# Transposing softmax probabilities by products with diagonals, or by true transposes with the reciprocals applied to y

## What is computed

```
scores = einsum('bhid,bhjd->bhij', q, k) + einsum('bhid,jd->bhij', q, rel)
scores = where(causal, scores, -inf)
probs  = softmax(scores, axis=-1)
y      = einsum('bhij,bhjd->bhid', probs, v)
out    = y.transpose(0, 2, 1, 3).reshape(b, t, c) @ w_proj + b_proj
```

## Time and profile before

| what | value |
|---|---|
| time, median of 3 runs | 7268.11 us (7267.75 to 7270.31) |
| span of the profiled execution, its own time | 7259.2 us |
| instructions | 167273 |
| PE / PEld busy | 91% / 82% |
| DVE / ACT / POOL busy | 74% / 50% / 43% |
| mean granted clock of TensorE | 0.906 |
| DMA | 24 GB/s over the span |
| products with diagonals (L714) | 1175.1 us of PE, 9216 instructions |
| diagonals (L502) | 608.4 us of POOL, 512 instructions |

### The profile page before, as it was taken

One profiled execution on the slowest core, in us unless ns is written; L12 is line 12 of the kernel. 1 busy time (PEld: TensorE's weight loads), 2 busy tenths in 40 slices (PEclk: granted clock), 3 DMA queues, 4 the chain that ended last, 5 costly groups with the idle time before them and its releaser, 6 DMA issues.

```text
span 7259.2 us, 167273 instructions
## 1 busy us (share of the span) xinstructions
PE 6605.1 (91%) x56000; PEld 5936.7 (82%) x56000; DVE 5383.8 (74%) x15934; ACT 3644.6 (50%) x12160; POOL 3111.4 (43%) x4048
## 2 busy tenths in 40 slices
PE   4999999999999999999999999999999999999998
PEld 4888888888888888888888888888888888888887
DVE  3777777777777777777777777777777777777776
ACT  1545555554555455545545554555455455545554
POOL 4444444444444444444444444444444444444443
PEclk8889899999899998989989998999899999899998
DMA  4211121112111111211121111112111211121110
GB/s 46 29 22 23 22 29 22 23 22 29 22 23 26 25 23 22 27 23 23 22 29 22 23 25 25 23 22 28 23 23 22 29 22 23 22 29 22 23 24 8
DMA packets 228657, 175.83 MB, mean 24 GB/s; under 512 B 27785, under 2 KB 228126, under 8 KB 228630
## 3 DMA queue, kind: packets, MB, share of 16 engines
q1 hardware_dynamic: 218934, 173.46, 18.4%
q10 hardware_dynamic: 8336, 1.07, 0.2%
q0 software_dynamic: 1360, 0.96, 0.1%
HBM read 156.11 MB, written 19.27 MB: 24 GB/s over the span
## 4 chain that ended last, share of the span: by engine, by line
issue 34%; PE 20%; DVE 18%; POOL 15%; POOLq 9%; DVEq 3%; ACT 1%; ACTq 0%
PE bank L693 7%; POOL diag L502 6%; DVE qz L1109 5%; POOL rstd L487 4%; PE bank L645 4%; DVE negmax L1128 2%; DVE z L1062 2%; PE bank L681 2%; POOLq L556 2%; POOL h L557 2%; PE bank L781 2%; POOLq L486 2%; POOL res L565 2%; PE bank L792 2%; POOLq L582 2%
## 5 line engine op out<-in xcount | busy, mean ns | idle before, releaser
L1514 ACT ACTIVATE p<-bank,negmax 98x98 f32<-98x98 f32 (+1 forms) x3072 | 1132.3, 376 | 317.6 <-DVE negmax L1128 274.6
L714 PEld LDWEIGHTS bank<-diag,p 128*98 128x98 f32 x9216 | 1066.0, 202 | 157.1 <-issue 104.0
L714 PE MATMUL bank<-diag,p 128*98 128x98 f32 x9216 | 1175.1, 291 | 14.7 <-POOL diag L502 1.7
L1522 ACT COPY pT<-bank 98x392 f32<-98x392 f32 x768 | 374.7, 488 | 1542.2 <-PE bank L714 1542.1
L693 PE MATMUL bank<-tokw,x_sb 128*98 128x193 f32 x4096 | 924.3, 382 | 9.1 <-DVEq L1049 9.1
L502 POOL TENSOR_TENSOR diag<-ident,rden 98x588 f32<-98x588 f32 x512 | 608.4, 1199 | 648.2 <-DVE rden L1142 648.2
L693 PEld LDWEIGHTS bank<-tokw,x_sb 128*98 128x98 f32 x4096 | 825.0, 260 | 67.5 <-issue 29.2
L1128 DVE TENSOR_REDUCE negmax<-bank 98x1 f32<-98x196 f32 (+2 forms) x1536 | 626.1, 456 | 269.0 <-PE bank L681 268.7
L681 PE MATMUL bank<-qk_parts,qz 128*98 128x196 f32 (+1 forms) x6144 | 744.7, 265 | 0.0
L681 PEld LDWEIGHTS bank<-qk_parts,qz 128*98 128x98 f32 x6144 | 656.8, 166 | 11.4
L520 POOL TENSOR_TENSOR qz<-qk_parts,ones 32x588 fp32r<-32x588 f32 x256 | 301.2, 1176 | 721.8 <-DVE qk_parts L1099 701.5
(11 more groups left out here) (272 smaller groups left out, 14889.4 us busy)
## 6 DMA issues: line engine op xcount, KB each, us to landing
x_sb<-in_x SPq DMA_DIRECT2D x384, 196.0 KB, 4.8
x_sb<-in_x SPq DMA_DIRECT2D x384, 189.0 KB, 8.0
out<-out_row SPq DMA_DIRECT2D x128, 147.0 KB
x_store<-in_L_tok_W SPq DMA_DIRECT2D x6, 96.0 KB
diag<-in_L_ffn_W SPq DMA_DIRECT2D x1, 576.0 KB
gstore<-in_L_ffn_W SPq DMA_DIRECT2D x1, 384.0 KB
p<-in_L_attn_w_attn ACTq DMA_DIRECT2D x2, 96.0 KB
gstore<-in_L_ffn_W ACTq DMA_DIRECT2D x1, 192.0 KB
```

The source lines that it names most:

```text
L714: last = mm(bank[b][0:HT, HT * i:HT * i + HT], src, diag[:, h // 3, t, h % 3], start=True, stop=True)
L1514: sc.activation((p1 if t else p0)[0:HT, 3 * s + g], bank[b][0:HT, c0:c0 + (T if t else HT)], ACT.Exp, bias=negmax[:, s, t, g:g + 1], accum ...
L1522: sc.copy(pt_dst(name[0], int(name[1:])), bank[RING[name]][0:HT, 0:4 * HT]).then_inc(sem["pT_act"], 1)
```

## The change

True transposes take the place of the products with diagonals. The diagonals on POOL (and their tile) go, and with them the four calls that waited for the sums of a slot each. DVE takes all reciprocals at once, after the copy of A0, and copies each 32 times beside itself (rden32, 98 x 768). PE transposes that in six blocks (R0 with four, R1 with two), ACT copies them to rdenT, in which each reciprocal stands in the 32 rows of its slot. In `attention` DVE multiplies y by rdenT to yn, ACT rounds yn instead of y, and DVE makes yparts from these. The ring has two more pieces, A4's copy moves from ACT to DVE, A3 now stands behind R0, and A4 with B1 ahead of the scatter. The semaphores rden_sb and diag_sb go; rden_T, rden32_sb, rdenT_sb and yn_sb are new. PE's A and B pieces now wait for `probs` itself. The tile norm_store takes diag's place, also for the weights that lie there during set-up.

```diff
@@ -54,11 +54,11 @@
-RING = dict(S0=0, S1=1, S2=2, T0=3, S3=0, S4=1, S5=2, S6=0, S7=1, A0=2, A1=0, A2=3, B0=1, A3=2,
-            B1=0, A4=1, A5=3, B2=0)
+RING = dict(S0=0, S1=1, S2=2, T0=3, S3=0, S4=1, S5=2, S6=0, S7=1, A0=2, A1=0, A2=3, B0=1, R0=2,
+            A3=0, B1=1, A4=3, R1=2, A5=0, B2=1)
 ORDER = list(RING)
 PT = [name for name in ORDER if name[0] in "AB"]
-PT_ACT = ("A1", "B0", "B1", "A4", "A5", "B2")
+PT_ACT = ("A1", "B0", "B1", "A5", "B2")
 PAIRS = ((0, 0), (0, 1), (1, 0), (2, 2), (2, 3))
...
@@ -190,7 +190,10 @@
         negmax = sb("negmax", [HT, 4, 2, NG])
         den = sb("den", [HT, 4, 2, NG])
         rden = sb("rden", [HT, 4, 2, NG])
-        diag = sb("diag", [128, 4, 2, NG, HT])
+        norm_store = sb("norm_store", [128, 2 * NG * T + 2 * NG * 128])
+        rdenT, yn = (norm_store[:, i * NG * T:(i + 1) * NG * T].rearrange("p (g t) -> p g t", g=NG)
+                     for i in range(2))
+        rden32 = norm_store[0:HT, 2 * NG * T:].rearrange("p (t g e) -> p t g e", t=2, g=NG)
         p0 = sb("p0", [128, NH, HT])
         p1 = sb("p1", [128, NH, T])
...
@@ -476,8 +479,7 @@
             select(diag_of[:], ALU.is_ge, 0.0, 31, -1, [[32, 4], [0, DH]])
             gp.drain().then_inc(one["consts_made"], 1)
             gp.wait_ge(one["w_ready"], 1)
-            for t in (p1, diag):
-                gp.memset(t[:], 0.0)
+            gp.memset(p1[:], 0.0)
             gp.drain().then_inc(one["p1_zeroed"], 1)
             def rstd(var, ve, r, name):
...
                     gp.tensor_tensor(h1b[:], h1[:], both(bp), ALU.add).then_inc(sem["h1b_sb"], 1)
-
-                def diagonals(s):
-
-                    gp.wait_ge(sem["rden_sb"], after("rden_sb", n, s + 1))
-                    gp.tensor_tensor(
-                        diag[0:HT, s].rearrange("p t g i -> p (t g) i"),
-                        ident[0:HT, 0:HT].unsqueeze(1).broadcast_to([HT, 2 * NG, HT]),
-                        rden[:, s].rearrange("p t g -> p (t g)").unsqueeze(2).broadcast_to(
-                            [HT, 2 * NG, HT]), ALU.mult).then_inc(sem["diag_sb"], 1)
...
@@ -530,8 +523,6 @@
                     gp.drain()
                     gp.tensor_tensor(sqsum[:].unsqueeze(2), x_sq[:, :, 0:1], x_sq[:, :, 1:2],
                                      ALU.add).then_inc(sem["sqsum_sb"], 1)
-                if front:
-                    diagonals(0)
                 if back:
                     gp.wait_ge(sem["sel_sb"], after("sel_sb", m))
...
@@ -539,17 +530,12 @@
-                    diagonals(1)
...
-                    diagonals(2)
-                    diagonals(3)
...
@@ -710,10 +696,20 @@
                     else:
                         blocks = [(4 * k + i, 1, 1) for i in range(4)]
                     for i, (h, t, u) in enumerate(blocks):
-                        src = p1[:, h, HT * u:HT * u + HT] if t else p0[:, h]
-                        last = mm(bank[b][0:HT, HT * i:HT * i + HT], src, diag[:, h // 3, t, h % 3],
-                                  start=True, stop=True)
+                        src = p1[0:HT, h, HT * u:HT * u + HT] if t else p0[0:HT, h]
+                        last = pe.transpose(bank[b][0:HT, HT * i:HT * i + HT], src,
+                                            ident[0:HT, 0:HT])
                     last.then_inc(sem["p_T"], 1)
+
+                def inverse_cols(k, b):
+
+                    for i, g in enumerate(((0, 1), (2,))[k]):
+                        for t in range(2):
+                            last = pe.transpose(
+                                bank[b][:, i * T + t * HT:i * T + t * HT + HT],
+                                rden32[:, t, g],
+                                ident[0:HT, 0:HT])
+                    last.then_inc(sem["rden_T"], 1)
                 def bank_free(name):
...
@@ -726,6 +722,8 @@
                         pe.wait_ge(sem["probs"], after("probs", n, int(o[1:]) + 1))
                     elif o[0] == "T" and head:
                         pe.wait_ge(sem["tok_y"], after("tok_y", l))
+                    elif o[0] == "R":
+                        pe.wait_ge(sem["rdenT_sb"], after("rdenT_sb", n, int(o[1:]) + 1))
                     elif o[0] in "AB":
                         engine, count = evacuation(o)
                         pe.wait_ge(sem[engine], after(engine, n, count))
@@ -742,10 +740,13 @@
                             by = "qz_sb" if k < 4 else "qz2_sb"
                             pe.wait_ge(sem[by], after(by, n, k // 2 % 2 + 1))
                         scores(k, RING[name])
+                    elif kind == "R":
+                        pe.wait_ge(sem["rden32_sb"], after("rden32_sb", n))
+                        inverse_cols(k, RING[name])
                     else:
                         s = (2 * k + 1 if kind == "A" else 4 * k + 3) // 3
-                        pe.wait_ge(sem["diag_sb"], after("diag_sb", n, s + 1))
+                        pe.wait_ge(sem["probs"], after("probs", n, 2 * s + 2))
                         transposes(kind, k, RING[name])
                 def embed(t, q0, q1):
...
@@ -852,6 +853,7 @@
                     pe.wait_ge(sem["pT_dve"], after("pT_dve", n))
                     pe.wait_ge(sem["pT_act"], after("pT_act", n, SEMS["pT_act"] - 1))
+                    pe.wait_ge(sem["rdenT_sb"], after("rdenT_sb", n))
                     for groups in ((0, 1), (2,)):
                         for g in groups:
                             for s in range(4):
...
                 if front:
+                    causal("R0")
                     causal("A3")
                 if back:
                     attn_out()
                 if front:
                     causal("B1")
+                    causal("A4")
                 if back:
                     scatter()
                 if front:
-                    causal("A4")
+                    causal("R1")
                     causal("A5")
                     causal("B2")
                     attention()
...
@@ -1136,10 +1140,15 @@
                     ve.tensor_copy(pt_dst(name[0], int(name[1:])),
                                    bank[RING[name]][0:HT, 0:4 * HT]).then_inc(sem["pT_dve"], 1)
-                def inverse_sums(s):
-
-                    ve.wait_ge(sem["probs"], after("probs", n, 2 * s + 2))
-                    ve.reciprocal(rden[:, s], den[:, s]).then_inc(sem["rden_sb"], 1)
+                def inverse_sums():
+
+                    ve.wait_ge(sem["probs"], after("probs", n))
+                    ve.reciprocal(rden[:], den[:])
+                    ve.drain()
+                    ve.tensor_copy(
+                        rden32.rearrange("p t g (s e) -> p (t g) s e", e=32),
+                        rden[:].rearrange("p s t g -> p (t g) s").unsqueeze(3).broadcast_to(
+                            [HT, 2 * NG, 4, 32])).then_inc(sem["rden32_sb"], 1)
...
@@ -1311,13 +1320,19 @@
                 def attention():
+                    def group(t, g0, gn):
+                        return t[:, g0:g0 + gn].rearrange("p g t -> p (g t)")
+
+                    for i, (g0, gn) in enumerate(((0, 2), (2, 1))):
+                        ve.wait_ge(sem["y_mm"], after("y_mm", n, i + 1))
+                        ve.tensor_tensor(group(yn, g0, gn), bank[2 + i][:, 0:gn * T],
+                                         group(rdenT, g0, gn), ALU.mult).then_inc(sem["yn_sb"], 1)
+                    ve.drain()
                     for i, (g0, gn) in enumerate(((0, 2), (2, 1))):
                         ve.wait_ge(sem["yhi_sb"], after("yhi_sb", n, i + 1))
                         ve.scalar_tensor_tensor(
-                            yparts[:, g0:g0 + gn].rearrange("p g t -> p (g t)"),
-                            yhi[:, g0:g0 + gn].rearrange("p g t -> p (g t)").bitcast(F32),
-                            lo_rows[:], bank[2 + i][:, 0:gn * T], ALU.mult,
-                            ALU.add).then_inc(sem["yparts_sb"], 1)
+                            group(yparts, g0, gn), group(yhi, g0, gn).bitcast(F32), lo_rows[:],
+                            group(yn, g0, gn), ALU.mult, ALU.add).then_inc(sem["yparts_sb"], 1)
                 def mlp_input():
                     ve.wait_ge(sem["h3_rstd"], after("h3_rstd", m))
...
@@ -1384,19 +1398,17 @@
                     mix_pooled()
                 if front:
                     maxima(6)
-                    inverse_sums(1)
                 if back:
                     max2()
                 if head:
                     patch_variance()
                 if front:
                     maxima(7)
-                    inverse_sums(2)
                 if head:
                     embedding()
                 if front:
                     transposed("A0")
-                    inverse_sums(3)
+                    inverse_sums()
                 if back:
                     mix_cols()
                     context2()
...
                     transposed("A3")
+                    transposed("A4")
                 if head:
                     h1_stats()
```

(16 more changed lines are left out.)

12 lines of the change are left out of this document (4 added, 8 removed).

## The result

The changed kernel takes 7146.8 us (median of 4 runs, 7144.6 to 7148.1), the kernel before 7269.0 on the same chip: ratio 0.983, 95% interval 0.9816 to 0.9844. It is faster; the forecast was slower, 7400.

The account below looks back on a forecast made before the run. PE, with its granted clock, was taken to set nearly all of a step's time. Short steps at 54.4 us and long at 56.7, half and half, plus 1.0 for patches: +1.1 x 127 - 2 = +137, 7400 us, own range 7300 to 7510.

Parts of the forecast that it names:

- The three terms of the short step: Mix 1.1 us earlier, A4's copy on DVE +0.46, y times reciprocals before the projection +1.03; together +0.4 us.
- A transpose is one record and 0.09 us: PE: each true transpose of 98 columns is one instruction of 0.09 us, against 0.17 a block for diagonal products.
- the wait for mT: PE's wait for DVE's split of mT ahead of the mix: still some 1.6 us, since PE comes earlier too.
- +2.5 us in a long step: Clock low through the transposes stays low at the projection (1.0 us) and the products behind it (1.5).
- the 1.5 us put on the short steps: One low-clock stretch behind PE's new idleness at the projection, taking short steps to 54.4 us.
- only grow: nothing: PE's waits for y_row's bank and mT grow as transposes before them shorten, so nothing is gained there.
- The short steps: Four of eight neighbouring steps, 52.5 to 54.3 us, clock low only some 3 us after the wait for mT.
- the fast rival: Clock granted as before: -1.0 us a step, 7140 us; chance 0.30.
- My own signs for right and wrong: Right: mean clock under 0.89, low at a later projection. Wrong: clock holds 0.906 or rises, or projection no later.
- My -2.7 for the longest step: From the mix to h2, PE's halved transposes at low clock shorten 17.2 to 15.6 us; with the 1.1, -2.7.
- "The change does not reach" the patches: Low stretch in the patch products, 1.6 us in five steps of eight: 1.0 us a step, before and after.
- The transposes' rule as a rival: Transposes neither raise nor hold the clock, so no step is short: +2.7 us a step, 7610 us; chance 0.17.

Follow-up runs that it names:

- run 13: Kernel before, GpSimd's multiplications kept, with six filler products ahead of the mix and four ahead of the token selection: 6767.7 us.
- run 7: Changed kernel with six filler products ahead of the mix and four ahead of the token selection: 6989.9 us.
- run 5: Changed kernel with six products of 128 columns filling PE's gap ahead of the mix, into an unread bank: 7136.5 us.
- run 6: Changed kernel with twelve transposes of 128 columns filling PE's gap ahead of the mix, into an unread bank: 7132.7 us.
- run 4: Changed kernel without the multiplication of y by the reciprocals, whose transposes and copies stay: 7139.7 us.
- the ninth run: Changed kernel with DVE's multiplication of y by the reciprocals moved ahead of the normalisation of h to f: 7212.1 us.
- run 10: Changed kernel with two of DVE's copies given to ScalarE, the reciprocals 32 wide and A4's: 6908.0 us.
- run 11: Changed kernel with y multiplied ahead of f and both copies (reciprocals 32 wide, A4's) on ScalarE: 6775.4 us.
- run 3: Changed kernel with each transpose of p issued twice into the same place: 7301.7 us.
- run 2: Changed kernel with products with the identity in place of the true transposes of p: 7143.9 us.
- run 8: Kernel before with constant diagonals, GpSimd's four multiplications a step left out, output not divided by the sums: 6691.9 us.
- run 1: Changed kernel with four multiplications of the diagonals' shape put back on GpSimd, into an unread tile: 7568.4 us.

## Why the prediction was wrong

The forecast added 1.1 us to a step, and 0.9 went. The terms of the chain held; the price put on the clock did not.

Means of the parts of a step in us. With both gaps filled, the kernel before has steps without any low clock (run 13) and the changed one 25 with under 1 us of it, at h2 alone (run 7): these show the change with the clock all but out of the way.

| part | before, no low | changed, under 1 us low | before, mix 10.2 | changed, mix 10.2 |
|---|---|---|---|---|
| h2 to y_row | 34.48 | 34.58 | 34.29 | 34.26 |
| y_row to mix | 5.53 | 4.46 | 5.53 | 4.45 |
| mix to merge | 5.13 | 5.65 | 8.19 | 7.67 |
| merge to f | 2.77 | 2.78 | 2.78 | 2.77 |
| f to projection | 2.07 | 3.07 | 3.34 | 3.16 |
| projection to h2 | 1.33 | 1.43 | 1.36 | 1.35 |
| step | 51.31 | 51.95 | 55.48 | 53.68 |

*The three terms of the short step were right.* The mix starts 1.07 earlier (-1.1), A4's copy costs 0.52 (+0.46), y times reciprocals 1.00 (+1.03). Between y_row and the projection, where neither column has any low clock, the change adds 0.46 us (+0.4 was reckoned). The whole step is 0.64 longer; the other 0.2 lies on both sides of h2, with the changed steps' rest of low clock.

*A transpose is one record and 0.09 us*: right, and so is the wait for mT, 1.46 us (1.6).

*The step that failed is the clock's*, in the long steps: "where the clock is low through the transposes, it is low through the projection and into the up products", +2.5 us in a long step. Low through the transposes it is, in every step and so oftener than I had it. But projection to h2 takes 1.37 us on average (1.34 before) and h2 to z 5.78 (5.92): of the 2.5 us neither the 1.0 nor the 1.5 is there. The stretch ends ahead of the projection or at it, after 10.2 or 13.7 us. I had put the new idleness in front of the projection; but PE comes late to that point, with attention products that ended only at 3589.8 in the step shown, and the steps sorted show no wait for f (but one of 0.1 us). The idleness is there only when the clock stays up: in runs 5 to 7, with PE waiting 1.94 us for f, the low stretch did come at the projection and cost 1.0 us in it, and in run 7, where it was 6.8 us long, 2.4 more from h2 to z (8.2 for 5.78). So the term was a real one, put on steps that could not have it. With the 1.5 us put on the short steps for the same idleness it makes 2.0 us a step on average, the whole distance from the forecast's +1.1 to the -0.9.

The new idleness that these steps do have lies ahead of the mix. The prediction said that the two waits there "only grow: nothing", which held for the chain, but it left them out of the clock: together they are 2.3 us for 1.8. Steps with a long stretch from the mix on were 122 of 122 with 2.3 us (also in runs 4 and 9), 57 with the 1.8 of the kernel before, 38 and 18 with 1.6 (runs 10 and 11), none once a filler stood there. Idleness is not all of it: run 3 had 48 such steps with 0.9 us and transposes twice, run 2 had 2 with 0.7 us and products. How idleness and transposes share it stays open.

*The short steps vanished*: not one has 3.4 us behind the mix. So the fast rival met the number (7140) and not the mechanism, since the clock was not granted as before. My own signs for right and wrong didn't tell the two apart either: the mean clock fell under 0.89 and the projection came later, as the forecast had it. Only the clock at the projection spoke against it.

*Where the gain is, then.* By the table of steps, a low stretch of 10.2 us at the mix costs the kernel before 4.17 us (55.48 - 51.31) and the changed one 1.73 (53.68 - 51.95); 13.7 us cost 5.61 and 2.64. (Counted only from the mix to the projection, where the steps compared have no low clock, 10.2 us cost 4.3 and 2.1.) I read three reasons. Behind the scatter 10 instructions run in it for 24: in run 3, with twice the transposes, 13.7 us cost 4.4 (58.49 - 54.08). A4's copy on DVE had already made mix to merge 0.5 longer, so that the stretch adds 2.0 there for 3.1; in run 10, with that copy back on ScalarE, 10.2 us add 2.5. And the multiplication of y comes after f, so that attention products ending late are hidden behind it: f to projection grows by 0.1 us where it grew by 1.3. The third is an argument from the rows alone. In sums over 122 steps: before, 65 stretches of 3.4 us at 1.26, 24 of 10.2 at 4.17, 33 of 13.7 at 5.61 and 85 in the patches at 1.65 make 4.2 us a step; after, 75 at 1.73, 47 at 2.64, 28 in the patches at 1.54 and 22 behind h2 at 1.48 make 2.7. So -1.46 for the clock and +0.64 for the chain (or -1.28 and +0.46, with the rest of low clock in run 7 taken out of the chain): -0.82 x 127 = -104, for the -122 measured. My -2.7 for the longest step was the right mechanism for this (58.83 to 56.31, or 56.07).

*"The change does not reach" the patches* was wrong too: the stretch there came in 85 steps before and in 28 after, 0.8 us a step, of which the 22 steps with the stretch behind h2 took 0.3 back. Filling the wait ahead of the selection removes it, so it needs that wait; why it comes in some steps, in all (run 4) or in few, with the wait the same 0.96 us in steps with it and without, was not settled.

*The transposes' rule as a rival* (7610) fell as well: by runs 2 and 3 they hold the clock less well, by runs 5 and 6 as well as products. What differs between the two places was not tried.

## What to carry to other kernels

Where a granted clock moves under a kernel, price a change twice: once at full clock, on its dependency chain, and once by what each low stretch costs at its place. Filling PE's two waits with products into an idle bank gave steps at full clock here, by which the change could be read, and was itself worth 7% on the kernel before, where the change was worth 1.7%. An engine freed is worth what its neighbours lose to it: GpSimd's four multiplications cost 1.8 us a step through DVE, and the work that replaced them cost 2.3 (0.75 ahead of the mix, 0.5 ahead of the merge, 1.0 ahead of the projection) until the copies were put on ScalarE and the multiplication of y into a wait; then steps without low clock took 49.82 us for 49.49 in run 8, 0.3 more. An instruction moved ahead in a queue brings its own wait along, as the ninth run shows.

## What was not expected of the hardware

GpSimd's multiplication slows more of DVE's operations than the subtractions of the earlier trace rows: in run 1 the cast of mT took 1.04 us for 0.26, not the subtraction alone. The Trainium skill, "SBUF — State Buffer", section "SBUF: two separate sides", has the two engines share a port pair that one of them locks for a whole instruction while the other waits. The rows fit that: 0.8 us more for the cast and 0.8 for the subtraction, each less than one multiplication of 1.19 us. A step often settled to 54.6 us, in three kernels with different chains (runs 4, 5 and 6), with its low stretches at the same places each time: a gain on the chain was paid back by a low stretch elsewhere until both gaps were filled. And a stretch of 13.7 us at 1.2 GHz, begun where PE had idled for 1.8 us, cost the kernel before 5.6 us a step, by the clock alone.
